# First layer of a four-layer convolution chain: when the next pair of channels is normalised, stored and loaded

## The reference

```python
def _conv_reflect(x, w, bias, dil, pad):
    xp = jnp.pad(x, ((0, 0), (0, 0), (pad, pad), (pad, pad)), mode='reflect')
    out = lax.conv_general_dilated(xp, w, rhs_dilation=(dil, dil), ...)
    return out + bias[None, :, None, None]

def _denoise_block(x, w1, b1, w2, b2, w3, b3, a, b, c):
    trip = _triplets(x)      # each channel with its neighbours before and after
    o = (a * _conv_reflect(xf, w1, b1, 1, 2) + b * _conv_reflect(xf, w2, b2, 2, 4)
         + c * _conv_reflect(xf, w3, b3, 4, 8))
    return jnp.tanh(o)

# --- layer 0 ---   _gn: group norm, 8 groups of 2 channels
y = _denoise_block(_gn(x), blk1 ...)
x = x + _denoise_block(y, blk2 ...)
# --- layers 1, 2, 3: quantised 3x3 conv, 17x17 box filter, 3x3 conv of the 2-D spectrum ---
```

## Time and profile before

| | us |
|---|---|
| median of 3 runs | 5379.86 |
| lowest and highest of them | 5368.85, 5382.81 |
| span of the profiled execution | 5383.9 |
| TensorE busy in it | 4994.9 |
| VectorE busy | 3365.2 |
| ScalarE busy | 2396.6 |
| matmuls of line 679, busy | 3027.2 |

### The profile page before, as it was taken

The page is one execution under the profiler, slowest core; times in us unless marked ns, Lnnn a source line. Parts: engine busy times, 40 slices in busy tenths (PEclk is TensorE's granted clock), DMA queues, the critical chain, the costliest instruction groups (busy, mean ns, idle before and its releaser), DMA issues. The chain is left out here.

```text
span 5383.9 us, 178367 instructions
## 1 busy us (share of the span) xinstructions
PE 4994.9 (93%) x78653; PEld 3092.8 (57%) x78653; DVE 3365.2 (63%) x6195; ACT 2396.6 (45%) x2999; POOL 1362.4 (25%) x1629
## 2 busy tenths in 40 slices
PE   4998999899899999999999997998777799999998
PEld 2444444444447569997666663443556466666665
DVE  5543444344342555555555546887999788888888
ACT  1222222222221111111111117885999689899997
POOL 0000000000001111111111100000777355555556
PEclk9999999999999999999999998999999999999999
DMA  8677777777666767667667657998688366666664
GB/s 246 217 228 235 224 228 232 223 223 237 222 209 199 226 200 239 207 203 236 203 208 236 205 178 277 321 325 302 256 308 309 129 152 152 150 150 153 151 152 120
DMA packets 366864, 1166.78 MB, mean 217 GB/s; under 512 B 60457, under 2 KB 61096, under 8 KB 287018
## 3 DMA queue, kind: packets, MB, share of 16 engines
q1 hardware_dynamic: 363928, 1152.98, 69.0%
q10 hardware_dynamic: 2162, 2.39, 0.2%
HBM read 683.58 MB, written 453.51 MB: 211 GB/s over the span
## 5 line engine op out<-in xcount | busy, mean ns | idle before, releaser
L679 PE MATMUL c_p<-c_w,wc 128*32 128x512 f16 x55296 | 3027.2, 381 | 91.1 <-DMA c_w<-xs 81.1
L679 PEld LDWEIGHTS c_p<-c_w,wc 128*32 128x32 f16 x55296 | 1896.0, 97 | 1194.4 <-DMA c_w<-xs 76.2
L739 ACT ACTIVATE c_t<-c_p,cbias,cscale 128x512 f32<-128x512 f32 x512 | 397.9, 777 | 2582.6 <-PE c_p L679 2582.6
L591 DVE TENSOR_SCALAR c_y<-c_t 128x512 f16<-128x512 f32 x256 | 109.2, 426 | 855.1 <-ACT c_t L739 854.1
L601 DVE TENSOR_TENSOR a_x<-c_t,a_x 128x512 f32<-128x512 f32 x256 | 221.3, 865 | 666.7 <-ACT c_t L739 658.5
L1699 PE MATMUL f_P<-f_qh,f_wt 64*64 64x512 f16 x4608 | 545.7, 378 | 1.8 <-DVE f_t L1595 1.8
L1699 PE MATMUL f_P<-f_hl,f_wt 64*64 64x512 f16 x4608 | 545.3, 379 | 0.0
L1860 POOL TENSOR_TENSOR f_y<-f_y,f_x 128x512 f32<-128x512 f32 x256 | 330.7, 1292 | 449.3 <-DVE f_hl L1574 443.2
L1595 DVE SCALAR_TENSOR_TENSOR f_t<-f_P,f_kk,f_ci 128x256 f32<-128x256 f32 x1024 | 423.4, 476 | 12.8 <-PE f_P L1699 7.6
L810 POOL COPY c_y<-c_y 128x16 f16<-128x16 f16 x512 | 85.6, 197 | 1360.7 <-DVE c_y L593 1360.7
L1459 POOL TENSOR_TENSOR e_hl<-e_g,e_hl 128x2048 f16<-128x2048 f32 x63 | 257.1, 4081 | 609.3 <-ACT e_hl L1409 609.3
(11 more groups left out here) (263 smaller groups left out, 5887.4 us busy)
## 6 DMA issues: line engine op xcount, KB each, us to landing
c_w<-xs SPq DMA_DIRECT2D x576, 264.0 KB, 5.6
c_w<-ys SPq DMA_DIRECT2D x576, 264.0 KB, 4.0
d_x<-x SPq DMA_DIRECT2D x128, 1024.0 KB, 7.6
x<-d_x SPq DMA_DIRECT2D x128, 1024.0 KB, 5.1
ys<-c_y SPq DMA_DIRECT2D x576, 132.0 KB
xs<-a_hl SPq DMA_DIRECT2D x70, 1056.0 KB, 9.8
a_x<-in_x SPq DMA_DIRECT2D x256, 256.0 KB, 6.8
a_x<-in_x SPq DMA_DIRECT2D x128, 512.0 KB, 5.2
```

Source lines behind the costliest of these rows:

```text
L679: t = p.matmul(pg[32 * j:32 * j + 32, :], wu[:, blk, wl, var, di, :], buf[:, bk, xl * PW + PAD + dx:xl * PW + PAD + dx + NW], start=(di == ...
L739: s.activation(tt_[n % 3][:, :], pp[:, n % 4, :], ACT.Tanh, bias=cbias[:, blk:blk + 1], scale=cscale[:, blk:blk + 1]).then_inc(c_act, 1)
```

## The change

**Steps by group number.** `stage_of` now takes n = 4u + g from a table. Pair 2 has its steps 2 and 3 at groups 0 and 1. A later pair i starts at `first_group(i)`, 64 * image + 4 + 7 * j, where image and j count from pair 3: groups 4, 11, 18, ... 53, then 68, and so on. A pair takes seven groups and no step stands in groups 57 to 67 of an image change. `load_x` for pair i stands at groups 4 and 6 after the start of pair i - 2.

**Signals.** `c_ld[half][g]` is one semaphore for each half and group, and every group waits for its own windows.

**Small products.** `p0` and `p1_` stand inside the next group, behind 60 of its 108 matmuls.

**Window loads.** Only unit 0 and the units with u % 16 == 2 are late; all others load at every group. The residual loads of block 2's first two units (`load_res`) stand at units 60 and 61 instead of 63 and 64.

**Weights of later layers.** `channel_weights` moves from group 11 to 9, its small products from behind groups 10 and 13 to behind 8 and 11, `scaled_weights` from group 19 to 15.

```diff
-        c_ld = [sem(f"c_ld{i}") for i in range(2)]
-        c_l0 = [sem(f"c_l0{i}") for i in range(2)]
+        c_ld = [[sem(f"c_ld{i}{j}") for j in range(4)] for i in range(2)]
...
-        def stage_of(u, g):
-
-            nxt, half = (u + 1) // 2 + 2, u % 2
-            return (nxt, (g + 2) % 4) if nxt < NG and g // 2 == half else (None, None)
+        def first_group(i):
+
+            image, j = divmod(i - 3, 8)
+            return 64 * image + 4 + 7 * j if i > 2 else -2
+
+        steps = {first_group(i) + z: (i, z) for i in range(2, NG) for z in range(4) if first_group(i) + z >= 0}
+        loads_x = {first_group(i - 2) + 4 + 2 * c: (i, c) for i in range(4, NG) for c in range(2)}
+
+        def stage_of(n):
+
+            return steps.get(n, (None, None))
...
-            return 128 * sum(1 + (place(r)[2] == 0) for r in range(u % 2, u + 1, 2) if r)
+            return 32 * sum(1 + (place(r)[2] == 0) for r in range(u % 2, u + 1, 2))
...
-                        if (u, g) == (2, 3):
+                        if (u, g) == (2, 0):
+                            mark["v"] = ch.n
+                        if (u, g) == (2, 1):
                             channel_weights()
-                        if (u, g) == (4, 3):
+                        if (u, g) == (3, 3):
                             scaled_weights()
...
-                    if u == 0:
-                        p.wait_ge(c_l0[g // 2], 128)
-                    elif g == 0:
-                        p.wait_ge(c_ld[half], n_win(u))
+                    p.wait_ge(c_ld[half][g], n_win(u))
...
+                        if di == 4:
+                            i, s = stage_of(n - 1)
+                            if s == 0:
+                                p0(i)
+                            if s == 1:
+                                p1_(i)
...
                         products(u, g)
-                        if s == 0:
-                            p0(i)
-                        if s == 1:
-                            p1_(i)
-                        if (u, g) == (2, 2):
+                        if (u, g) == (2, 0):
...
-                        if (u, g) == (3, 1):
+                        if (u, g) == (2, 3):
...
-                                             [[CP, 16], [RW, 2], [1, 4 * RW]])).then_inc(c_ld[half] if u else c_l0[g // 2], 16)
+                                             [[CP, 16], [RW, 2], [1, 4 * RW]])).then_inc(c_ld[half][g], 16)
...
-                    late = u < NU and half == 0
+                    late = u < NU and u % 16 == 2 or u == 0
...
-                        if g == 0 and NU <= u + 1 < 2 * NU:
+                        if g == 0 and NU + 2 <= u + 1 < 2 * NU:
                             load_res(u + 1)
-                        if g == 1 and u // 2 + 4 < NG:
-                            load_x(u // 2 + 4, (half,))
+                        if g == 0 and u in (NU - 4, NU - 3):
+                            load_res(u + 4)
+                        if n in loads_x:
+                            load_x(loads_x[n][0], (loads_x[n][1],))
```

More of the change, by code:

```diff
@@ L634, in _ @@
                     for g in range(4):
-                        i, s = stage_of(u, g)
+                        i, s = stage_of(4 * u + g)
                         if i is not None:
                             (v0, v1, v2, v3)[s](i)
-                        if (u, g) == (2, 3):
+                        if (u, g) == (2, 0):
+                            mark["v"] = ch.n
+                        if (u, g) == (2, 1):
                             channel_weights()
-                        if (u, g) == (4, 3):
+                        if (u, g) == (3, 3):
                             scaled_weights()
-                        if (u, g) in ((2, 2), (3, 1)):
-                            mark["v", u] = ch.n
                         if table_of(u) is not None and g % 2 == 0:
@@ L707, in _ @@
                     for g in range(4):
-                        i, s = stage_of(u, g)
                         products(u, g)
-                        if s == 0:
-                            p0(i)
-                        if s == 1:
-                            p1_(i)
-                        if (u, g) == (2, 2):
+                        if (u, g) == (2, 0):
                             p.wait_ge(w13_ld, 160)
-                            p.wait_ge(a_v, mark["v", 2])
+                            p.wait_ge(a_v, mark["v"])
                             p.matmul(pq[:, 0:432], rep[:, :], w16[:, :, :].rearrange("p j n -> p (j n)"), start=True, stop=True).then_inc(w13_p, 1)
-                        if (u, g) == (3, 1):
+                        if (u, g) == (2, 3):
                             p.wait_ge(a_v, mark["g3"])
-                            p.wait_ge(a_v, mark["v", 3])
                             p.matmul(pq[:, 0:1], ones[:, :], c2b[:, 0:1], start=True, stop=True).then_inc(w13_p, 1)
@@ L762, in _ @@
                     for g in range(4):
-                        i, st_ = stage_of(u, g)
+                        i, st_ = stage_of(4 * u + g)
                         if st_ == 2:
                             root_step(s, a_v, mark["rt", i], a_rt, ve, sq)
-                        if (u, g) == (4, 3):
+                        if (u, g) == (3, 3):
                             root_step(s, a_v, mark["sv"], w13_rt, c2b[:, 1:2], c2b[:, 2:3])
@@ L902, in _ @@
                     blk, b, p, half = place(u)
-                    late = u < NU and half == 0
+                    late = u < NU and u % 16 == 2 or u == 0
                     for g in range(4):
-                        i, s = stage_of(u, g)
+                        n = 4 * u + g
+                        i, s = stage_of(n)
                         if s == 3:
```

## The result

| | before | after |
|---|---|---|
| median of 4 runs each, us | 5381.34 | 5306.66 |
| lowest and highest | 5368.85, 5394.03 | 5304.04, 5316.0 |
| span of the profiled execution | 5383.9 | 5306.8 |
| ratio after to before, 95% interval | | 0.9863 (0.9846 to 0.9881) |

The change wins 75 us. Forecast were 5239 and a range of 5226 to 5284: the sign was right, about half of the gain is missing, and the time lies above the range. In the profiled executions the miss is 5306.8 - 5243.2 = 63.6 us.

What follows compares the result with a forecast made beforehand. The prediction took TensorE at 5.835 us a group to bound the first layer. Its terms 40.0 + 84.1 + 9.9 + 6.7 = 140.7 us took the profiled 5383.9 to 5243.2, median 5239, range 5226 to 5284.

Steps and rivals of the forecast that it cites:

- What bounds the kernel: First layer: TensorE is the engine never idle, at 5.835 us a group.
- the sum of 181.3 us: First layer, groups 0 to 263: all time over 5.835 us a group, the most a reordering could win, barring an earlier start.
- the two causes: First layer's losses: small products, 2.32 us a pair, and TensorE's waits for windows, mainly at image changes.
- Small products, 40 us: Inside the next group, a pair's two products cost 0.84 instead of 2.32 us; 27 pairs win 40 us.
- Windows and image changes, 84.1 us: Three image changes: earlier stores and loads at each group remove the window waits, winning 84.1 of 99.3 us.
- windows still late: Rival at image changes: each keeps 8 us of wait and 1.8 behind it, 30 us return, 5269 us; chance 0.12 to 0.13.
- signs of being wrong: First layer: a `c_w` wait behind group 16, a small-product group over 6.4 us, or later layers changing length.
- the best sign: Block 2, 2072 to 2119 us: same doubled windows loaded group by group, TensorE busy 47.00 of 47.00 us.
- Block 2's start, 9.9 us: Groups 208 to 263: waits for each group and earlier unit 64 loads remove the 9.9 us beyond small products.
- The start, 6.7 us: Groups 0 to 16: layer starts at 70.0, part is lost again; 6.7 us left at group 16, between 3 and 12.
- The long wait in group 5: Start: TensorE idles 8 us for statistics of pair 3's late x; the small product runs at 112.1.
- Layers 1 to 3: Layers behind the first: shifted and otherwise unchanged.

Runs made afterwards that it cites:

- e5_before_y16: The kernel before with the y stores' two outer destination counts exchanged, so they run on sixteen engines (output not the reference's): 5281.5 us, ratio 0.9809.
- e9_before_unit_store: The kernel before with only the y stores changed: a unit's stores issued together by strip, on sixteen engines: 5287.54 us, ratio 0.9828.
- e1_y16: The changed kernel with the y stores' two outer destination counts exchanged, so they run on sixteen engines (output not the reference's): 5248.56 us, ratio 0.9751.
- e6_small_only: The kernel before with only the small products moved inside the next group, behind 60 of 108 matmuls: 5372.89 us, ratio 0.9975.
- e11_x3_again: The changed kernel with unit-wise y stores on sixteen engines and pair 3's x loaded ahead of unit 1's windows, rerun on another chip: 5242.35 us.
- e8_unit_store_x3: The changed kernel with unit-wise y stores on sixteen engines and pair 3's x loaded ahead of unit 1's windows: 5239.86 us, ratio 0.9743.

## Why the prediction failed, point by point

**What bounds the kernel: right, with a wrong cause.** TensorE's 5.835 us a group and the sum of 181.3 us over it held, and so did the first of the two causes, the small products. The second didn't: image changes were put on late and bundled windows, and `e5_before_y16` shows that the y stores make 80 of their 99 us, and most of the rest is small products.

**Small products, 40 us: right in size.** 6.26 us for a group with a product against 7.74 and 6.25 in the earlier trace rows, no idle time before it between image changes, and 46 to 47 us by the medians in the runs whose stores use sixteen engines. The middle of an accumulation costs the same 0.42 as a boundary. "`p1_` has a whole group for three short instructions" counted these instructions, and not what stands ahead of them in VectorE's order and what that waits for.

**Windows and image changes, 84.1 us: the failed step.** It is the sentence that sets 346 GB/s asked against 300 to 312 at full share and finds the burst "5 to 8 us late against 41 us of room", and the next one, "groups 64 to 71 then ask for only 160 GB/s". Both spread every byte over 16 engines. By the four that carry all y stores it is 9.2 us asked in 5.83 and then 5.4 to 5.9 in 5.83. What came was 84.1 - 54.5 = 29.6 us. The windows themselves were in time for groups 64 to 79, and evictions 5.83 us apart through groups 57 to 68, as forecast. Between 9 and 11 us of each image change were late y tiles, which no step and no rival named. The other 8 to 9 were late windows for groups 80, 144 and 208, near the 9.8 us each that the rival "windows still late" had, and SP's order is in its list; the four engines that held SP back are not. It had 30 us where 54.5 were missing. Two of the prediction's own signs of being wrong came: a wait for `c_w` behind group 16, and groups with a small product over 6.4 us, group 70 with 16.3. The 0.13 of that rival and the upper end of 5284 rest on the same mean over 16 engines. The block 2 stretch of the earlier trace rows, called "the best sign", was none: block 2 stores no y.

**Block 2's start, 9.9 us: right in size, wrong in cause.** 208 to 263 loses 2.5 us, and there is no wait for windows at units 64 and 65. But the late loads and the wait for a whole unit, which the prediction held responsible, are still there in `e5_before_y16` and `e9_before_unit_store`, and those lose only the 6.9 us of three pairs' small products. So the y stores alone made these 9.9 us. The changed order gets round them as well, so the number came out; that is in part luck.

**The start, 6.7 us: the long wait right, 6.4 us off.** TensorE here, first three pieces of the loop:

```profile
73.83 34.36 PE L682 MATMUL c_p<-c_w,wc 128*32 128x512 f16 x600 [3.87 <-DMA c_w<-xs]
114.30 0.59 PE L662 MATMUL a_p<-a_mv,ones 128*128 128x1 f32 x2 [6.10 <-DVE a_mv L425]
...
132.91 6.02 PE L682 MATMUL c_p<-c_w,wc 128*32 128x512 f16 x108 [1.64 <-DMA c_w<-xs]
```

The long wait in group 5 is there (product forecast at 112.1, measured 114.30), and a small one before group 8. What the prediction didn't see is that the 9.87 us before group 8 of the kernel before were the y stores (0.80 in `e5_before_y16`). In `e1_y16` group 0 starts at 69.94 (70.0 forecast), the product stands at 111.23 and the start loses 20.0 us (20.1 forecast). So 2.6 of the 6.4 us are the y stores again; the other 3.8 were lost before group 0. The first store of a pair is issued at 40.03 here and at 40.11 in `e6_small_only`, at 43.23 in `e11_x3_again`, and between 36.72 and 37.33 in the kernel before and the nine other profiles. The same kernel has 36.96 (`e8_unit_store_x3`) and 43.23 (`e11_x3_again`), so this is a difference from one execution to the next, here of 3.3 us; what makes it is open.

**Layers 1 to 3: right to 2.1 us,** which comes and goes (2141.0 us here, 2137.8 in `e1_y16`, 2138.9 before).

**The sum.** With the one cause taken away and nothing else, `e1_y16` gives a span of 5242.7 us where 5243.2 was forecast. Part of that closeness is luck: stretches are off by up to 0.8 us with both signs, and the median of `e1_y16`, 5248.56, lies 4 us above its profiled run. The terms of 84.1 and 9.9 us were the right amounts to win, put on the wrong cause.

## What to carry to other kernels

Before a sum over transfers is made against the rate of all DMA engines, ask of each transfer how many engines it runs on. The access pattern says so by its outermost counts, the page by a missing landing time and the packet count, and the DMA view by plateaus of the share at a low digit. A mean share of 0.5 can be made of stretches with all sixteen busy and stretches with four full and twelve idle.

When an instruction is moved to where its own input is just in time, look at the whole queue of the engine that makes the input, and at what that engine can be held up by. And when a part of a change wins far less alone than beside another edit, as the products' 13 us alone and 46 with stores on sixteen engines, another bound stands behind it; look for that first.

## What the hardware showed

- Transfers of 64 pieces of 2112 bytes on four engines move 90 to 107 GB/s together and on two 49 to 55; each engine that takes part adds one packet to the queue's count (362776, 363928, 366232 and 370840 for 2, 4, 8 and 16).
- The four engines seem to be the same for every y store: with several stores issued and not landed the share stays on its plateau of 2, where other engines for the next one would lift it to 5. No run here names the engines.
- With its DMA engines behind, SP issues more slowly: three y stores take 3.47 us to issue and two windows 1.74, against 1.86 and 1.19 in `e1_y16`. It is not the access pattern: in the changed kernel two y stores at 341.44 us, away from image changes, take 1.19.
- The small float32 product costs 0.42 us in the middle of an accumulation, as between two.
- What lies ahead of the first store of a pair takes 36.7 to 37.3, 40.1 or 43.2 us, with the same kernel too. A profile's span carries that difference, and an effect of 3 us has to be read behind it.
